# Four-stage transformer block on one core: the attention's output bias added in four pieces by GpSimd beside the diagonal tiles

## The reference, cut to what matters

```python
x = _layernorm(x + _L0_attn_ref(x, ...))   # linear attention, 16 heads      -> stage A
x = _layernorm(x + _L0_ffn_ref(x, ...))    # gated feed-forward in fp8       -> stage B
x = _layernorm(x + _L1_attn_ref(x, ...))   # causal softmax attention        -> stage C
x = _layernorm(x + _L1_ffn_ref(x, ...))    # base matrix and routed experts  -> stage D

def _L1_attn_ref(x, Wq, bq, Wk, bk, Wv, bv, Wo, bo):
    q = x @ Wq + bq
    k = x @ Wk + bk
    v = x @ Wv + bv
    scores = einsum('bqd,bkd->bqk', q, k) / sqrt(128)       # causal mask, -inf above the diagonal
    weights = softmax(scores)
    return einsum('bqk,bkd->bqd', weights, v) @ Wo + bo
```

## Time and profile before

| what | value |
|---|---|
| median of 3 runs | 1561.22 us (1559.19 to 1561.75) |
| the profiled execution's own time | 1564.32 us |
| its span, first to last instruction | 1562.6 us |
| PE busy | 1475.6 us, 94% |
| DVE busy | 1005.5 us, 64% |
| ACT busy | 736.5 us, 47% |
| POOL busy | 341.0 us, 22% |
| mean granted TensorE clock | 0.982 of full |

### The profile page before, as it was taken

How to read it: one execution, slowest core, us unless ns; L and a number is a source line. 1 busy time by engine, 2 the same in 40 slices (tenths; PEclk the granted TensorE clock), 3 DMA queues, 4 the chain that set the end, 5 groups by cost and what they waited for, 6 DMA issues and landing times.

```text
span 1562.6 us, 23839 instructions
## 1 busy us (share of the span) xinstructions
PE 1475.6 (94%) x9484; PEld 1012.5 (65%) x9484; DVE 1005.5 (64%) x1961; ACT 736.5 (47%) x1040; POOL 341.0 (22%) x256
## 2 busy tenths in 40 slices
PE   8999999999999977899999999977999999989998
PEld 6677777777777755344555555455666666557886
DVE  3355545464545545988778777843888888556665
ACT  4333333333333322977877886743434444442333
POOL 0021112121111222000000000000666776750001
PEclk9999999999999989999999999989999999999999
DMA  7203131303122140001100110022100000000112
GB/s 262 79 27 107 33 101 53 105 28 106 51 83 64 42 169 21 28 1 55 55 27 28 54 55 0 1 68 81 39 1 1 1 1 1 1 1 28 55 54 81
DMA packets 43904, 79.93 MB, mean 51 GB/s; under 512 B 7073, under 2 KB 14881, under 8 KB 42386
## 3 DMA queue, kind: packets, MB, share of 16 engines
q1 hardware_dynamic: 43794, 78.41, 14.8%
HBM read 53.24 MB, written 25.17 MB: 50 GB/s over the span
## 4 chain that ended last, share of the span: by engine, by line
PE 58%; issue 22%; DVE 14%; ACT 3%; POOL 2%; DMA 0%; SPq 0%; DVEq 0%; POOLq 0%; ACTq 0%
PE psum L142 12%; PE psum L144 11%; PE psum L143 11%; PE psum L1328 5%; DVE sm L465 3%; PE psum L612 2%; PE psum L1306 2%; PE psum L638 2%; PE psum L633 2%; PE psum L989 2%; PE psum L627 2%; PE psum L982 1%; DVE c_mx L1249 1%; PE psum L642 1%; PE psum L647 1%
## 5 line engine op out<-in xcount | busy, mean ns | idle before, releaser
L982 PE MATMUL psum<-early,high 128*128 128x512 fp8e4 x1024 | 234.5, 381 | 11.5 <-DVE low_r L954 4.2
L982 PEld LDWEIGHTS psum<-early,high 128*128 128x128 fp8e4 x1024 | 98.0, 98 | 133.9 <-ACT early L863 6.7
L1182 POOL TENSOR_TENSOR c_ls<-c_ls,c_pr 128x512 f32<-128x512 f32 (+2 forms) x136 | 162.3, 1193 | 57.4 <-ACT c_pr L1225 48.0
L411 POOL TENSOR_TENSOR rms<-ms,mhalf 128x16 f32<-128x16 f32 x32 | 93.2, 2911 | 365.6 <-DVE ms L474 365.6
L1225 ACT ACTIVATE c_pr<-c_sc 128x512 f32<-128x512 f32 (+2 forms) x144 | 85.3, 594 | 151.5 <-DVE c_sc L1264 139.4
L142 PE MATMUL psum<-Qh,Kh 128*128 128x512 f32 (+1 forms) x272 | 142.4, 523 | 0.0
L1328 PE MATMUL psum<-c_pr,V 128*128 128x512 f32 (+2 forms) x288 | 138.1, 565 | 3.1 <-ACT c_pr L1225 1.9
L1264 DVE TENSOR_TENSOR c_sc<-psum,c_mb 128x512 f32<-128x512 f32 (+2 forms) x144 | 92.2, 642 | 50.1 <-PE psum L144 37.5
L989 PE MATMUL psum<-high,b_act 128*128 128x512 fp8e4 x512 | 115.2, 379 | 0.0
L142 PE MATMUL psum<-early_r,high_r 128*128 128x512 f32 x256 | 106.7, 417 | 5.8 <-DVE early_r L437 5.8
L143 PE MATMUL psum<-Ql_r,Kh 128*128 128x512 f32 (+1 forms) x272 | 105.6, 388 | 0.0
(11 more groups left out here) (227 smaller groups left out, 3253.7 us busy)
## 6 DMA issues: line engine op xcount, KB each, us to landing
low<-x_dram SPq DMA_DIRECT2D x9, 1024.0 KB, 5.6
wst<-in_L_ffn_w_gating SPq DMA_DIRECT2D x16, 512.0 KB, 4.6
xs<-in_L_attn_x SPq DMA_DIRECT2D x8, 1024.0 KB, 8.0
xt<-in_x_turned SPq DMA_DIRECT2D x7, 1024.0 KB, 4.8
x_dram<-xs SPq DMA_DIRECT2D x7, 1024.0 KB, 4.7
x_dram<-low SPq DMA_DIRECT2D x5, 1024.0 KB, 4.3
wst<-in_L_ffn_w_linear SPq DMA_DIRECT2D x16, 256.0 KB, 4.8
high<-x_dram SPq DMA_DIRECT2D x4, 1024.0 KB, 6.8
```

Of the source, the lines that this page charges most:

```text
L411: nc.gpsimd.tensor_tensor(rms[:, :], ms[:, :], const["mhalf"][:, 0:H], ALU.pow).then_inc(*done)
L982: last = t.matmul(out[:, h, :], w8g[:, tile + k, (2 * m + h) * P:(2 * m + h + 1) * P], x8[:, u, k, :], start=k == 0, stop=k == DC - 1)
L1182: nc.gpsimd.tensor_tensor(ls[:, i % 2, q0:], ls[:, i % 2, q0:], pr[:, g % SLOTS, q0:], ALU.add).then_inc(*L.done(*name))
```

## The change

The addition of bo becomes four of 128x512, `("bo", i, c)`, placed in block i itself, each behind the `sum` of a diagonal tile; `y` of chunk c waits for its own piece. The bias matmul and its DVE addition become an ordinary job `bias` behind the first `mb`. And the stages' lists are joined by one `plan` of jobs instead of places written out per engine: `pieces` cuts each engine's list behind the same job. Quoted here are the parts that say this; the rest of the diff renames and moves the tables of banks.

```diff
-    order = max_jobs(0) + [("mb", 0)]
+    order = max_jobs(0) + [("mb", 0), ("bias", 0)]
...
             pool_order.append(("sum", *name[1:]))
+            if name[2] >= tiles(i) - CH:
+                pool_order.append(("bo", i, name[2] - tiles(i) + CH))
         elif kind == "L":
             act_order.append(("oh", i))
             dve_order += [("ol", i), ("rl", i)]
-            pool_order += [("bo", i)]
...
             elif kind == "bo":
-                if i < here:
+                if i == 0:
+                    wait_for(pool, 0, (V, ("bias", 0)))
+                c = name[2]
+                if i < here and c == 0:
                     pool.wait_ge(x_in[i], 16)
-                else:
+                elif i >= here:
                     wait_for(pool, 0, (prev["A"], ("norm", i, CH - 1)), (prev["M"], ("x2", i, 1)))
-                nc.gpsimd.tensor_tensor(xs[i], xs[i], bo[:, None, :].broadcast_to([P, CH, D]), ALU.add).then_inc(*L.done(*name))
+                nc.gpsimd.tensor_tensor(xs[i][:, c, :], xs[i][:, c, :], bo[:, :], ALU.add).then_inc(*L.done(*name))
...
-                wait_for(dve, 0, (M, name), (L, ("bo", i)), (V, ("rl", i)))
+                wait_for(dve, 0, (M, name), (L, ("bo", i, c)), (V, ("rl", i)))
...
-        splits = [(3, 0)] + [(6, 3 * k) for k in range(DC + 1)]
+        plan = part("A", None, ("o", last, 3))
+        plan += part("B", None, ("x", 0, 1)) + part("A", ("o", last, 3), ("y", last, 2))
+        plan += part("B", ("x", 0, 1), ("u", 0, 0)) + part("A", ("y", last, 2), None)
+        plan += part("B", ("u", 0, 0), ("VT", last - 1)) + [("C", ("ahead", "dve", 0))] + part("B", ("VT", last - 1), None)
+        plan += [("D", ("ahead", "pool", 0))]
+        splits = {("s", 3, 2): 0, **{("s", 6, 3 * k + 2): k + 1 for k in range(DC + 1)}}
+        for job in part("C", None, ("y", last - 1, CH - 1)) + part("C", ("y", last - 1, CH - 1), ("L", last)):
+            plan.append(job)
+            if job[1] in splits:
+                plan += [("D", ("ahead", "act", splits[job[1]])), ("D", ("ahead", "dve", splits[job[1]]))]
+        plan += part("D", None, ("x", 0, DC - 1)) + part("C", ("L", last), None) + part("D", ("x", 0, DC - 1), None)
...
-                n = 0
-                for piece, (i, k) in enumerate(splits):
-                    m = upto(C["act_order"], ("exp", i, k))
-                    C["scalar"](act, C["act_order"][n:m])
-                    D_["scalar_ahead"](act, piece)
-                    n = m
+                for stage, names in pieces(plan, stages, "act"):
+                    stage["scalar_ahead" if isinstance(names, int) else "scalar"](act, names)
```

More of the change, by code:

```diff
@@ L102, in wait_for, with cuts_of, plan_banks, pieces @@
         eng.wait_ge(*steps.at(block, *name, back=back))
[L105 to L137, removed]
+def cuts_of(job_counts):
+    return {job: dict(zip(("pe", "act", "dve", "pool"), counts)) for job, counts in job_counts}
+def plan_banks(plan, stages):
+    last = {}
+    for s, job in plan:
+        stage = stages[s]
+        if job not in stage["banks"]:
+            continue
+        use = stage["uses"][job]
+        banks = stage["banks"][job]
+        stage["free"][job] = [last[w] for w in banks if w in last and last[w] != use]
+        for w in banks:
+            last[w] = use
+def pieces(plan, stages, engine):
+    at = {s: 0 for s in stages}
+    run, stop = None, 0
+    for s, job in plan:
+        if run is not None and (s != run or job[0] == "ahead"):
+            yield stages[run], stages[run][engine][at[run]:stop]
+            at[run], run = stop, None
+        if job[0] == "ahead":
+            if job[1] == engine:
+                yield stages[s], job[2]
+        else:
+            run, stop = s, stages[s]["cuts"][job][engine]
+    if run is not None:
+        yield stages[run], stages[run][engine][at[run]:stop]
 def split3(tensor, out, hi_w, lo_w, hi_x, lo_x, first, last):
@@ L584, in tensor_engine @@
                 m = name[2] if len(name) > 2 else 0
[L585 removed]
+                u, out = b % 2, bank_of(*name)
                 tokens = slice(m * P, (m + 1) * P)
[L587 removed]
+                needs = free[name]
                 if (kind, b) == ("q", 0):
@@ L964, in tensor_engine @@
                 t = nc.tensor
-                needs = [free[name]] if name in free else []
+                needs = free[name]
                 u = b % 2
@@ L1141, in stage_c, with bank_of @@
             w, n_m = (3, 4, 7)[n_m % 3], n_m + 1
-        bank_of[name] = w
-        steps, step = reader[name[0]]
-        if w in last_use and not (name[0] == "pv" and name[2] > 0):
-            free[name] = last_use[w]
-        last_use[w] = (steps, (step, name[1]) if name[0] in ("pv", "L") else (step, *name[1:]))
+        steps, step = reader[kind]
+        banks[name] = (w,)
+        uses[name] = (steps, (step, i) if kind in ("pv", "L") else (step, *name[1:]))
+    def bank_of(*name):
+        return bank[banks[name][0]]
     def load_ahead(sp):
@@ L1295, in tensor_engine @@
                 pe.wait_ge(pro_dve, 7)
-                wait_for(pe, 0, prev["last_use"][4])
-                nc.tensor.matmul(bank[5][:, :], bvw, wof, start=True, stop=True).then_inc(pro_pe, 1)
-            out = bank[bank_of[name]]
-            if name == ("pv", 0, 0):
-                pe.wait_ge(pro_dve, 8)
-            needs = [free[name]] if name in free else []
-            if kind == "mx":
+            out = bank_of(*name)
+            needs = free[name]
+            if kind == "bias":
+                wait_for(pe, 0, *needs)
+                last = nc.tensor.matmul(out[:, :], bvw, wof, start=True, stop=True)
+            elif kind == "mx":
                 q, k = name[2:]
```

280 lines of the change are left out of this document (123 added, 157 removed).

## The result

The changed kernel takes 1578.8 us (median of 4 runs, 1575.8 to 1580.1) against 1561.5 us for the kernel before: the ratio is 1.0111, with a 95% interval of 1.0092 to 1.0130. It is about 17 us slower, where 8.1 were forecast, and the time lies above the range.

The account below looks back on a forecast made before the run. TensorE, busy 1475.6 of 1562.6 us, was taken as the bound. Terms -2.3 - 1.3 + 1.3 + 5.4 + 3.3 + 1.7 + 0 = +8.1 us gave 1572.4, less 3.1 a median of 1569.3 us; range 1560.5 to 1575.

Parts of the forecast that it names:

- `bo` off the first `y`: Stage C: first `y` no longer waits for `bo`; -2.3 us over blocks 1, 2, 4, 5, -1.3 in block 7.
- ScalarE's copies: Blocks 6 and 3: VectorE's weight pieces wait for copies two tiles later; +5.4 us, and +1.3 net of `bo`'s 0.9.
- the step that let TensorE keep nearly half of pieces 4 and 5 in hand: Block 6: of 4.0 us VectorE loses on these pieces, TensorE loses a little over half, +2.3 us.
- The tail, +3.3: Block 7: three pieces ahead of the last `sum` delay it and `L` by 3.3 us, bounds 0 to 3.9.
- all that follows is one chain: Behind block 7's late last `sum`: nothing seen to hide the delay, so the whole 3.3 us counts.
- The bias matmul, 0: Start of stage C: pair of 1.02 us moves behind the first `mb`; 0 us, between -0.4 and +0.4.
- A meets B, +1.7: B's first four VectorE instructions ahead of A's last `ol`: wait 2.16 becomes 4.4 us, `tanh` wins back 0.52; +1.7 us.
- I count no further change: Behind the `ol` wait where A meets B: clock at 0.58 of full over 3 us, no further change counted.
- From span to median: Whole kernel: profiled execution lay 3.1 us above the median, so 1572.4 became a median forecast of 1569.3 us.
- Rival D: Longer and added gaps bring three more half-clock stretches of 1.3 us: +3.9 us, 1573.2 us; chance 0.15.

Follow-up runs that it names:

- pieces only: Kernel before with nothing but `bo` in four pieces among the diagonal sums; copies, bias and gelu at their old places: 1559.7 us, 0.9994.
- TensorE given work there: Changed kernel with stage D's four transposes ahead of block 7's `L`: 1570.8 us, 1.0068.
- one piece ahead: Changed kernel with one piece of block 7's `bo` ahead of its last sums and three behind the last: 1572.4 us, 1.0073.
- copies back: Changed kernel with ScalarE's six pieces of stage D's weights two tiles earlier again, VectorE's pieces staying: 1567.1 us, 1.0032.
- bias back: Changed kernel with bias matmul ahead of the first `mx` and its addition behind the last maximum, as before: 1574.3 us, 1.0075.
- gelu back: Changed kernel with VectorE's list of stage A run out before stage B's begins, as before: 1575.4 us, 1.0089.
- VectorE's pieces later: Changed kernel with VectorE's six pieces of stage D's weights two tiles later as well, ScalarE's as changed: 1565.0 us, 1.0021.
- The tail's step: Changed kernel with block 7's four pieces of `bo` behind its last `sum`, blocks 0 to 6 as changed: 1570.4 us, 1.0059.

## Why the prediction was wrong

The direction was right, and so was the list of costs but for the bias; the sum was half of what came. By its own steps:

- **`bo` off the first `y`.** Right where it acts: -0.6, -0.6 and -0.7 in blocks 1, 4 and 5, -1.8 in block 7. It failed in block 2 by 1.2 us, because the step counted what the pieces free and not what they come to lie beside.
- **ScalarE's copies.** The mechanism was right, and the run with VectorE's pieces moved as well shows it. Of the size, +6.2 and +1.6 were measured against +5.4 and +1.3. In block 6 the loss is 3.4 us up to its `rstd` (1301.23 before, 1307.61 now), which stands behind piece 3; for the first three pieces 3.1 were forecast. The other 2.8 stand against 2.3: the step that let TensorE keep nearly half of pieces 4 and 5 in hand was too kind. In block 3 the agreement is luck. With the copy put back the block is still at +0.5, where the forecast's `bo` alone gave -0.9; the copy cost 1.0 and not 2.2, and a second portion of half clock, which the kernel with pieces only (-1.2 there) did not have in its trace, goes with the rest.
- **The tail, +3.3.** The wait came out at 3.1. The step that failed is the one behind it, that "all that follows is one chain": the chain was taken over at its durations of full clock. Behind the longer gap `L` and the transposes ran at half, and stage D's first matmuls lost two portions instead of one: +6.0. The runs with TensorE given work there, and with one piece ahead, point to the clock and not the delay for nearly half of it. So do traces of the same tail: with the wait of 3.1 us each time, it cost 4.0 to 4.3 us where one portion followed the wait (copies back, bias back, pieces only) and 5.7 to 6.0 where two did (the changed kernel twice, gelu back, VectorE's pieces later). At 2.7 us this is the largest miss by place.
- **The bias matmul, 0.** Wrong, and outside its own bounds. It was weighed as TensorE time moved from one place to another. But at the new place VectorE's 0.69 us stand behind it and ahead of the first `sub`, and the pair runs at half clock, 1.91 us instead of 1.02. In the trace +1.7; putting it back gave 2.8 by place and 4 to 5 in the runs, adding it alone 1.2 in the runs and 1.8 by place.
- **A meets B, +1.7.** The wait grew by exactly the 2.25 us of the sum. The failed step is "I count no further change" of the clock: half clock follows the old gap in a third of the traces and the new one in all. That is two thirds of a portion more, 1.1 us, and makes it 2.8, an estimate; putting the gelu back gave about 3, adding it alone 1.6, and the runs do not tell the two apart.
- **From span to median.** Of the 9.5 us between forecast and result 5.3 are the sum's. The other 4.2 are the distances of the two profiled executions from their medians: the one before lay 3.1 above (1564.3 against 1561.2), the changed kernel's 1.1 below (1577.7 against 1578.8). The prediction took the 3.1 off again, as if whatever was peculiar to that execution were in the changed kernel's too. The half clock behind the gap of 2.16 us was peculiar to it, since six of nine traces with that gap have none, and in the changed kernel it comes every time. It is not all: the trace before also lost 3.4 us of clock near 50 us, where 14 of the 18 traces lost 1.7. What makes up the 4.2 beyond this stays open.

Rival D, more half clock for +3.9 us, had a chance of 0.15 beside the forecast. It came together with the forecast, since the waits that the forecast counted are the gaps that half clock follows. The two were one case, and the range had no room for it.

What stays open is why the steps taken back one at a time give some 27 us by their ratios (the changed kernel taken at 1.01075, the mean of its two) where 17 were lost. An estimate from the intervals leaves some 7 to 8 us of doubt on this excess of 10, since all four differences share the changed kernel's own. The copies, the bias and the gelu do add up: 11.8, 5.1 and 2.9 us make 19.8, and undoing all three gave 17.7. The tail's step gave 7.6 us in the changed kernel and 3.2 with the others undone; in the traces the tail itself differs by 2.0 us between the two, with 6.8 us of lost clock in the one and 3.4 in the other: a portion less behind the wait and a portion less at stage D's start. Whether this depends on when the tail comes, or differs from one execution to the next, no run shows: none shifted the tail alone, and only the changed kernel has two traces, which agree.

## What to carry to other kernels

Price a new wait of the engine that sets the time twice, once as the gap and once as what runs behind it at the lower clock, and keep both in one case. Of an operation that is moved, look at what it comes to stand between and what runs beside it there, down to the smallest instruction. Where a producer is moved towards its reader, look whether the reader can move with it: here that took the whole cost of the part away.

## What the runs showed of the hardware

- Up to stage D's last block, lost clock came in portions of 1.7 us: 27.3 us or 16 of them in the trace before, 35.7 us or 21 in the changed kernel's.
- The same gap of 2.16 us was followed by half clock in three traces of nine, the gap of 4.41 us in nine of nine, and the wait of 3.1 us for the last `sum` in seven of seven, by one portion in three of them and by two in four. A profiled execution shows one case of this, and the runs of the kernel before range over 6 us (1558.7 us at a mean granted clock of 0.987 to 1564.7 at 0.982, in 24 runs).
- `TENSOR_SCALAR` on 128x4 with one tensor read from SBUF took 1.04 us beside a GpSimd addition of 1.27 us (in another kernel 1.18 beside four in a row), 0.17 without.
